# Two-layer decoder kernel on one core: x loaded in four pieces, pair 1's norms in the attentions' openings, VectorE's work for a coming pair spread over banks, and expert slots that place before they multiply

## The reference, cut to what matters

```python
x = x + L0_attn(layernorm(x))            # 16 heads of 16, alibi, causal, batch 8, 256 tokens, width 256
x = x + L0_xattn(layernorm(x), ctx)      # one head of 256, 64 context rows + 256 own rows
x = x + L0_moe(layernorm(x))             # 8 experts, top 2, hidden 512
x = x + L1_attn(layernorm(x))            # 16 query heads, 4 key/value heads, causal
x = x + L1_xattn(layernorm(x), ctx)      # 16 heads over 8*64 context rows, fake-quantised q, k, v, weights
x = x + L1_moe(layernorm(x))             # 16 experts, top 4, hidden 128, plus a shared expert
```

## Time and profile before

| what | value |
| --- | --- |
| median of 3 runs | 1454.43 us (1453.02 to 1455.04) |
| the profiled execution | 1454.35 us, its span 1452.5 us |
| mean granted TensorE clock | 0.899 |
| PE busy | 1222.0 us (84%) |
| DVE busy | 898.3 us (62%) |
| ACT busy | 675.1 us (46%) |
| POOL busy | 462.4 us (32%) |
| memory | 123.43 MB, mean 85 GB/s |

### The profile page before, as it was taken

How to read it: one execution, slowest core, us unless ns; L and a number is a source line. 1 busy time by engine, 2 the same in 40 slices (tenths; PEclk the granted TensorE clock), 3 DMA queues, 4 the chain that set the end, 5 groups by cost and what they waited for, 6 DMA issues and landing times.

```text
span 1452.5 us, 25939 instructions
## 1 busy us (share of the span) xinstructions
PE 1222.0 (84%) x8255; PEld 846.7 (58%) x8255; DVE 898.3 (62%) x2622; ACT 675.1 (46%) x1412; POOL 462.4 (32%) x708
## 2 busy tenths in 40 slices
PE   4789998994799999768898868788788779899988
PEld 3467766773466666435565535555555555677755
DVE  3646664666232223367676578999999874555557
ACT  2245544331211111115444479999999981433310
POOL 1000101345511111201212134466655554355510
PEclk8799999996899999869899978887877878999999
DMA  8764752312111111153442030000000003344454
GB/s 154 165 135 118 159 135 80 111 45 81 53 44 48 48 45 45 55 155 107 105 130 70 3 120 2 2 31 31 28 20 24 24 31 131 110 143 146 147 175 142
DMA packets 71873, 123.43 MB, mean 85 GB/s; under 512 B 12614, under 2 KB 54982, under 8 KB 68239
## 3 DMA queue, kind: packets, MB, share of 16 engines
q1 hardware_dynamic: 59740, 91.76, 24.5%
q0 software_dynamic: 10272, 28.39, 5.6%
q10 hardware_dynamic: 1728, 1.61, 0.3%
HBM read 77.14 MB, written 44.19 MB: 84 GB/s over the span
## 4 chain that ended last, share of the span: by engine, by line
PE 52%; issue 13%; ACT 10%; DVE 10%; DMA 7%; POOL 6%; SPq 2%; POOLq 0%; DVEq 0%; ACTq 0%
PE ps L227 16%; PE ps L1086 14%; PE ps L1103 7%; ACT work L1800 5%; DMA W<-q_parts 3%; POOL xs_scratch L1417 2%; ACT work L1805 2%; PE ps L1071 2%; PE ps L1095 2%; DVE work L580 2%; PE ps L444 2%; PE ps L464 2%; POOL work L1831 2%; PE ps L479 1%; PE ps L1651 1%
## 5 line engine op out<-in xcount | busy, mean ns | idle before, releaser
L1086 PE MATMUL ps<-W,work 128*128 x628 | 228.2, 496 | 5.4 <-issue 4.5
L1800 ACT ACTIVATE work<-ps,work 128x512 f32<-128x512 f32 x256 | 211.5, 875 | 9.1 <-POOL work L1831 7.5
L1435 POOL DMA_INDIRECT ys_scratch<-work x118 | 113.2, 959 | 273.1 <-DVE work L1342 173.1
L1328 DVE TENSOR_TENSOR work<-work,ps 128x128 f32<-128x128 f32 (+1 forms) x118 | 49.7, 421 | 228.4 <-ACT work L1398 228.4
L1736 DVE TENSOR_REDUCE work<-ps 128x1 f32<-128x512 f32 x256 | 173.4, 681 | 28.3 <-PE ps L1645 27.0
L580 DVE TENSOR_REDUCE work<-ps 128x2 f32<-128x512 f32 (+1 forms) x192 | 128.0, 685 | 84.3 <-PE ps L447 83.7
L683 ACT ACTIVATE work<-ps 128x512 f32<-128x512 f32 x192 | 113.0, 601 | 109.4 <-PE ps L467 105.5
L1086 PEld LDWEIGHTS ps<-W,work 128*128 128x128 f32 x628 | 110.8, 191 | 75.5 <-issue 70.1
L271 POOL TENSOR_TENSOR rstd<-ve,half 128x1 f32<-128x1 f32 x96 | 56.4, 591 | 305.3 <-DVE ve L267 302.9
L1805 ACT COPY work<-ps 128x1024 bf16<-128x1024 bf16 x128 | 141.2, 1103 | 7.4 <-PE ps L1651 7.3
L1831 POOL TENSOR_SCALAR work<-work 128x1 f32<-128x1 f32 x256 | 99.6, 389 | 133.2 <-DVE work L1736 116.9
(11 more groups left out here) (253 smaller groups left out, 2358.4 us busy)
## 6 DMA issues: line engine op xcount, KB each, us to landing
work<-xs_scratch SPq DMA_DIRECT2D x79, 132.0 KB, 2.2
W<-ys_scratch SPq DMA_DIRECT2D x16, 512.0 KB, 3.9
q_parts<-work SPq DMA_DIRECT2D x48, 128.0 KB, 1.7
W<-k_parts SPq DMA_DIRECT2D x48, 128.0 KB, 4.5
W<-q_parts SPq DMA_DIRECT2D x16, 384.0 KB, 6.6
W<-in_w_in SPq DMA_DIRECT2D x6, 1024.0 KB, 11.1
work<-xs_scratch SPq DMA_DIRECT2D x39, 130.0 KB, 2.1
W<-q_parts SPq DMA_DIRECT2D x16, 256.0 KB, 7.0
```

The source lines that it names most:

```text
L1086: mm = q.e.matmul(PS[bks[c]][:, 0:N], self.XT[s % 2][:, k, :], w[:, k, bass.ds(regs[s] + 512 * c if c else regs[s], N)], start=k == 0, sto ...
L1435: q.e.indirect_dma_start(YS[L], bass.IndirectOffsetOnAxis(ap=self.dst[n % self.NY], axis=0), self.YB[n % self.NY], None).then_inc(*landing ...
L1800: q.e.activation(self.ee[n // 2 % 3][:, 512 * (h % 2):512 * (h % 2) + 512], PS[banks.of["c1_s", t, h]][:, :], ACT.Exp, bias=self.nb[:, h:h ...
```

## The change

It has five parts. x comes in four loads (tiles 0-1, 2-3, 4-7, 8-15) where there were three (0-1, 2-7, 8-15); the load of tiles 2-3 moves ahead of b_v's, that of tiles 4-7 takes the place of tiles 8-15's, and the latter goes, with w_o0, b_o0 and w_xa, into the entry of i = 0. The norm of pair 1 (with its adds in layer 1) is issued in the opening of each attention, straight after that of pair 0. In the iterations from -1 on, one tile's work stands in each unit: adds at u = 0 and 1, statistics at 2 and 3, powers at 3 and 4, norms at 6 and 7; `ln_turn` moves to u = 9 and `ln_copy` to u = 10. In the experts' slots, `dve_place` comes ahead of the wait for silu.

```diff
@@ x_ready
-            return [at("x" if t < 2 else "x1" if t < 8 else "x2", 0) if s == 0 else None,
+            return [at(("x", "x1", "x2", "x2", "x3", "x3", "x3", "x3")[t // 2], 0) if s == 0 else None,
@@ Attention.tensor
-                        if u == 7 and self.next_ln(i):
+                        if u == 9 and self.next_ln(i):
                             ln_turn(q, *self.next_ln(i), rp)
@@ Attention.vector
                 ln_stats(q, self.ln, 0)
                 ln_norm(q, self.ln, 0)
+                if L == 1:
+                    experts[0].add(q, 2)
+                    experts[0].add(q, 3)
+                ln_stats(q, self.ln, 1)
+                ln_norm(q, self.ln, 1)
                 q.wait_ge(*self.base())
                 e.memset(self.NPw, 0.0).then_inc(*q.step())
...
-                        if u == 2 and self.next_ln(i):
+                        if self.next_ln(i) and i > -2:
                             s, p = self.next_ln(i)
-                            if s == 3:
-                                experts[0].add(q, 2 * p)
-                                experts[0].add(q, 2 * p + 1)
-                            ln_stats(q, s, p)
-                        if u == 5 and self.next_ln(i):
-                            ln_norm(q, *self.next_ln(i))
+                            if s == 3 and u < 2:
+                                experts[0].add(q, 2 * p + u)
+                            if u in (2, 3):
+                                ln_stat(q, s, 2 * p + u - 2)
+                            if u in (6, 7):
+                                ln_norm1(q, s, 2 * p + u - 6)
@@ Attention.scalar
-                        if u == 8 and self.next_ln(i):
+                        if u == 10 and self.next_ln(i):
                             ln_copy(q, *self.next_ln(i))
@@ Attention.gpsimd
                 ln_pow(q, self.ln, 0)
+                ln_pow(q, self.ln, 1)
                 q.wait_ge(*self.base())
...
-                    if self.next_ln(i):
-                        s, p = self.next_ln(i)
-                        ln_pow(q, s, p)
                     for u in range(12):
+                        if u in (3, 4) and self.next_ln(i) and i > -2:
+                            s, p = self.next_ln(i)
+                            ln_pow1(q, s, 2 * p + u - 3)
                         self.beside(i, u, kv)
@@ Experts.dve_slots
+                        self.dve_place(q, s)
                         q.wait_ge(at("silu", L, s))
                         q.e.tensor_tensor(self.Ub[s % 2], self.Ub[s % 2], src, ALU.mult).then_inc(*up("u", L, s))
-                        self.dve_place(q, s)
@@ sync_program
             e.dma_start(b_qk[0], I["b_qk0"]).then_inc(*landing("w_att", "qk"))
+            e.dma_start(x[:, 2:4, :], xd[:, 2:4, :]).then_inc(*landing("x1", 0))
             e.dma_start(b_v[0], spread("b_v0")).then_inc(*landing("w_att", "b"))
             attention[0].sp_rows(q)
-            e.dma_start(x[:, 2:8, :], xd[:, 2:8, :]).then_inc(*landing("x1", 0))
...
             attention[0].sync(q, [
-                [late(x[:, 8:16, :], xd[:, 8:16, :], "x2", 0)],
+                [late(x[:, 4:8, :], xd[:, 4:8, :], "x2", 0)],
+                [],
                 [late(w_o0, rows_of("w_o0"), "w_o0", "w"), late(b_o0, spread("b_o0"), "w_o0", "b"),
-                 late(w_xa, rows_of("w_xa0"), "w_xa", "w")],
-                [late(ctxT[:, :, :], rows_of("ctxT"), "w_xa", "T"), late(b_m0, spread("b_m0"), "w_xa", "m"),
-                 late(w_r0, rows_of("w_r0"), "w_xa", "r")] +
-                [late(XS[0][8 * RS:8 * RS + 128, :], zt[0], "dummy", 0)],
+                 late(w_xa, rows_of("w_xa0"), "w_xa", "w"), late(ctxT[:, :, :], rows_of("ctxT"), "w_xa", "T"),
+                 late(b_m0, spread("b_m0"), "w_xa", "m"), late(w_r0, rows_of("w_r0"), "w_xa", "r"),
+                 late(x[:, 8:16, :], xd[:, 8:16, :], "x3", 0), late(XS[0][8 * RS:8 * RS + 128, :], zt[0], "dummy", 0)],
                 *[[w] for w in win]])
```

## The result

The changed kernel takes 1434.45 us, the median of 4 runs (1430.22 to 1436.32), against 1454.74 for the kernel before: a ratio of 0.985 with a 95% interval of 0.983 to 0.988, so 20 us faster. The direction is right; the forecast gain is less than half of the measured one. A second measurement with 5 runs gave 1433.48 us and 0.984 (0.980 to 0.987).

The account below looks back on a forecast made before the run. TensorE was read as busy 84% of the span, so gains could come only where it waits; -1.9 + 0.8 - 2.2 - 2.9 - 1.2 - 1.5 = -8.9 from 1454.35 gave 1445.4 us, range 1436.0 to 1453.5.

Parts of the forecast that it names:

- place first in layer 1: Layer 1's expert slots: place moves into VectorE's wait for silu, loads issued up to 1.1 us earlier; 1.5 us gained.
- Spreading: Layer 1's attention: 0.64 us in each of iterations 1, 2 and 4, 0.15 in 0 and 3; 2.2 us gained.
- the hand walk: Layer 1's attention, iteration 2, VectorE's order timed: unit 5 starts only 0.64 us earlier, the wait divided.
- The clock: Layer 1's attention: a quarter of the 11.9 us lost in five low-clock stretches comes back; 2.9 us gained.
- my formula: Layer 1's attention, five low-clock stretches: TensorE loses (1 - clock) x length, 11.9 us together.
- Layer 0's slots: Start of layer 0's expert slots: half of the 2.46 us wait for load 3 goes; 1.2 us gained.
- The rival in which place gets past the memset: Layer 0's slots: place runs beside GpSimd's memset, 2.46 us gained instead of 1.2, total 1444.2 us; chance 0.12.
- The loads of x: Layer 0's opening: smaller load of x and pair 1's earlier norm bring its parts sooner; 1.9 us gained.
- the pile: Layer 0's attention, iteration 0: 3.29 MB in 8 issues ahead of pair 1's `mrow` delays it; 0.8 us lost.
- The rate of 340 GB/s: Layer 0's opening: rate assumed for the load of x, so 0.5 MB less is 1.5 us.
- Layer 1's opening: Pair 1's parts ready about 5 us earlier, but transfers bound the writes; gain 0, bounds 0 and 1.2 us.
- the clock stays up throughout: Layer 1's attention, rival: 11.9 us of clock come back instead of 2.9, total 1436.4 us; chance 0.12.

Follow-up runs that it names:

- all but place: Changed kernel with dve_place put back behind the multiply; 1445.34 us, 0.992 of the kernel before.
- spreading: Kernel before with only adds, statistics, powers and norms spread over the units from iteration -1 on, turn and copy moved with them; 1445.84 us, 0.994.
- openings: Kernel before with only the four loads of x, the load order behind them and pair 1's norms in both openings; 1452.54 us, 0.999.
- TensorE at work: Kernel before with unit 5's attend scores repeated ten times in iterations 1, 2 and 4 of layer 1's attention; 1450.19 us, 0.998.
- only place first: Kernel before with only dve_place moved ahead of the wait for silu, in both layers; 1442.06 us, 0.991.
- no pile: Changed kernel with w_o0, b_o0 and w_xa back in the entry of i = -1; 1433.59 us, 0.984 of the kernel before.
- the version that goes further: Changed kernel with a fifth load buffer in layer 1 and the coming pair's work further apart; 1427.56 us, 0.984; with six weight loads later too, 1429.18 us.

## Why the prediction was wrong

Means over the profiles take out a good part of the clock's chance. Layer 1's slots: 144.6 in the five kernels with the old order and four buffers (before, all but place, spreading, openings, TensorE at work), 133.2 in the four with place first (after twice, only place first, no pile). Layer 1's attention: 158.5 in the six with the old block, 151.6 in the five spread as in the change. Layer 0's slots 218.8 and 215.7; layer 0's attention 169.7 and 167.2. That is 11.4 + 6.9 + 3.1 + 2.5 = 23.9 us, where the forecast had 1.5 + 5.1 + 1.2 + 1.1 = 8.9. The medians fell by 20 us in the first measurement and by 24 in the second. What lies outside the four stages varies by some us between profiles (758.7 before, 759.4 and 764.1 in the two of the changed kernel).

**The step that failed: place first in layer 1** (1.5 us, bounds 0 and 3; measured 11.4). Its mechanism was right: loads issued up to 1.1 us earlier, measured 1.3. Its price was read from one row, "TensorE waits 2.1 us for such loads, and after each wait a little for its own sequencer". The little was the main thing. As I read it, a late load stops TensorE's sequencer at the transposes while the array still works off what is queued; the gap appears a few instructions later, ahead of the weight load of the up-projection, and is put down to "issue": 11.7 us in 31 waits. The slots of the kernel before, taken one by one (5 to 77), agree: of the 24 loads that landed under 0.6 us ahead of their transposes, 20 are followed by such a gap of over 0.2 us; of the 41 that landed 0.7 us or more ahead, none is. With the 4.1 us put down to the loads, that is 15.8, and 3.8 are left after: 12 us, the measured gain within 1. The sum of the two rows follows the slots' time in all fourteen profiles: 15.3 to 17.5 us where the slots take 143.3 to 146.2, 11.0 at 140.4, 2.8 to 4.7 at 132.5 to 134.5. My upper bound of 3 should have been these 15.8.

**Spreading** (2.2 us, too small; in the mean of the profiles together with the clock 6.9 for 5.1). At full clock the hand walk is near: iteration 1 takes 23.95 us with the old block (and TensorE's repeats) and 23.51 spread, iteration 3 23.02 and 22.64, so 0.4 us each, for the 0.64 and 0.15 forecast. With one fall in either kernel it is worth more, and there the walk falls short: iteration 0 goes from 24.2 to 23.2, iteration 1 from 25.6 to between 23.8 and 24.0, iteration 2 from 22.8 to 21.4, iteration 4 from 25.4 to between 24.2 and 24.4. I had 0.15 for iteration 0 and 0.64 for each of the others. That the block's wait and slow matmuls no longer stand one behind the other would explain it; no run tests that. With the clock's 1.9 us (below) taken off the 6.9, spreading gave 5.0 in the mean, for 2.2.

**The clock** (2.9 us, bounds 0 and 11.9). The full price was read nearly rightly. By my formula iterations 1 to 4 lost 1.7 + 3.4 + 3.4 + 1.7 = 10.2; at full clock they are 101.1 - 92.2 = 8.9 us shorter (profile of before against that with TensorE at work; without the repeats iterations 2 to 4 take the same there, to 0.01 us). The quarter that I expected back was too little for this profile: falls in iterations 0, 1 and 3 are gone, those in 2 and 4 are there. I argued from `Cross1` that a divided wait would keep the clock low; with the change itself iterations 2 and 4 fall in every profile, but in the version that goes further, waits up to 1.3 us leave it at 1.00 in all five iterations. Against the mean of executions a quarter was nearer: by the same formula the falls cost 7.4 us in the mean of the six profiles with the old block and 5.5 in the five spread ones, 1.9 less.

**Layer 0's slots** (1.2, bounds 0 and 2.46; measured 3.1). The rival in which place gets past the memset is what happened: 0.22 us inside the memset against 2.87 inside the adds, and slot 3 without a wait. By the Trainium skill's page SBUF — State Buffer (section Who interferes with whom), a GpSimd instruction that only writes SBUF does not contend with a VectorE instruction of two SBUF inputs; the trace agrees in seven of the eight profiles with place first. In the eighth, the changed kernel again, place(0) starts 0.57 us before the memset's recorded end and takes 0.63, beside the first of the adds. The 0.6 us above the wait itself is within what these stretches vary (215.2 to 216.1, and 218.2 to 220.0).

**The loads of x** (1.9) and **the pile** (+0.8). Stack 1 gained 1.6 and stack 2 kept 1.0; the stage gained 2.5 in the mean, part of it by the spreading (168.6 with that alone). The rate of 340 GB/s does not follow from w_xa's row as I read it (1.44 MB in 5.4 us are 267 GB/s), but the trace of before has 352 GB/s from 35.0 to 38.3 us, where the load of x drains, so the 1.5 us stand. The pile delayed `mrow` by 5 us without a wait: 0 instead of 0.8. I had the rows land at 88.7; they landed near 87.1, ahead of their use.

**Layer 1's opening** (0). Right: the last write of pair 1 lands 21.1 us behind the first of pair 0, before 20.7, and with the weights out of its way, in the version that goes further, 16.7 without gain.

The rival "the clock stays up throughout" named 1436.4 us, near the result, but for a reason that holds only in part: two falls are still there, and the larger sum came from the slots. It is luck that it came so near. What is open is why an iteration of the same code falls in one execution and not in another, and why the spread iterations 2 and 4 always fall; no run here shows what decides it.

## What to carry to other kernels

- A late input does not show where it is waited for. TensorE showed most of it here as "issue" time further on, in the weight loads' row; bound the gain of an earlier release by all waits of both rows in the stretch, not by those that name the releaser.
- Where a ring of buffers is just deep enough, the release of a buffer is worth more than it looks: here 0.13 us of it moved 4 us over 79 slots, and one more buffer did as much as the reordering.
- Read the clock's losses in several executions before you price them; and spread a block on another engine as evenly as its due times allow, since one long wait costs its own time and can cost the clock behind it. Then look at the stages whose clock was full already: the widest spreading here took 6 us from layer 1's attention and gave 2 back in layer 0's.

## What the runs showed of the hardware that I had not expected

- With 40 matmuls repeated in a wait, iteration 1 of layer 1's attention was shorter in the one profile of that kernel, 23.95 us for 25.6: the granted clock stayed at 1.00 where six other profiles show 0.93.
- One iteration of unchanged code took 26.05 us at a mean clock of 0.87 in one execution and 23.02 at 1.00 in another.
- SP's queue held the issue of one transfer for 8.19 us with seven loads issued just ahead of it, and for 3.66 with four. Whether their number or their bytes decide it, no run here shows.
